# One-hot operations set apart in the attention's step, block factors written in two halves

## The chip, the core and the metric

The kernel runs on one core of a Trainium2 chip. The metric is the device time of one execution in microseconds (us). The engines work in parallel, each on its own queue in order, and meet by semaphores: TensorE multiplies, VectorE and ScalarE compute elementwise, GpSimd issues the gathers here, and SyncE issues the other transfers.

## The reference

Four graph layers follow each other on 3125 nodes of 128 features and 53125 edges, sorted by their destination `dst`. Each layer's output is added to its input and normalised:

```python
x = _layernorm(x + _L0_gnn_ref(x, edge_index, edge_type_16, ...))   # 2 bases
x = _layernorm(x + _L1_gnn_ref(x, src, dst, edge_type_32, ...))     # two layers, 4 bases each
x = _layernorm(x + _L2_gnn_ref(x, edge_index, W, b))                # sum of neighbours, linear, relu
x = _layernorm(x + _L3_gnn_ref(x, Wq, bq, ..., src, dst))           # attention, 8 heads

# inside L1, for each of its two layers:
msg = sum(comp[l][etype][:, b:b+1] * (h[src] @ basis[l, b]) for b in range(4))
h = tanh(segment_sum(msg, dst) + h @ loop_w[l] + bias[l])

# inside L3:
s = einsum('edh,edh->eh', q[row], k[col])
p = exp(s - segment_max(s, row)[row]);  attn = p / segment_sum(p, row)[row]
out = segment_sum(attn * v[col], row)
```

## The kernel before

The edges lie in 416 chunks of 128. The kernel runs three passes of edge sums (the first for L0, the second and the third for the two layers of L1; L2 is made of edge counts that the passes also collect) and then the attention. Times of the trace: first pass to about 540 us, second from 545 to 965, third from 965 to 1390, attention from 1460 on.

**A pass.** GpSimd fetches the source rows of a chunk by one indirect DMA (line 748), two chunks to a group, into a ring of 26 slots (G). VectorE writes for each chunk the scatter factors S (line 1404: position of the edge's destination in a window of 24, times the edge's coefficient for each base). TensorE multiplies G by S into `p_g` (line 815, `sums`), and VectorE adds that to `agg` (line 1431, `add`). A slot of G is refilled after its `sums` (GpSimd waits on `s_mm`).

The second and third passes are "mixed": of every 16 groups 12 are gathered this way, and the edges of the other four are handled as a block. For each of 13 blocks, 14 buckets of edges are picked out of the node table in SBUF by TensorE (line 931) and copied by ScalarE (line 1174). For each bucket VectorE writes the block factors `Sb` (lines 1434 to 1441, `block_factor`): four bases of a window of 72, 288 values to a partition, from the constant row `con` (places 1 to 72), the bucket's place `row[:, PAY - 2]` and its four coefficients. TensorE multiplies (line 944, `block_sum`), which increments `s_bs2`. `Sb` is a ring of 4. That makes 182 block factors in a pass, 364 in all.

VectorE's order in a step i of a pass (`sums_body`, one step a group): add of group i-3, block add where a block ends, count adds (line 1522), scatter factors of group i, block factors of step i+1, key one-hots for the counts (line 1508), and in the third pass residual, normalisation, splits and dense adds (line 1598) instead of the counts. TensorE's order: bucket fetch, block sums of step i, sums of group i-1, counts, transposes and products of finished tiles, in the third pass dense products (line 873).

**The attention** takes 26 batches of 16 chunks, each in four quarters of 4 chunks. GpSimd gathers key and value rows of a chunk (line 2021) into a ring of 64; it refills a slot when the quarter's `values` is done. VectorE multiplies queries and keys (`products`, line 2275), sums by head (`head_part`, line 2281), makes running maxima over a segment (`chunk_max`, `row_max`, `segment_max`), weighs the values (`values`, line 2334), and adds window sums to `agg` (`add`, line 2362). For the window sums TensorE needs the one-hot of each edge's place in a window of 40, `oh1`, a ring of 5 batches. `one_hots(k)` writes those of batch k in four operations of 4 chunks each, in step k-2, one right behind the other. Each increments `s_oh1`, and TensorE's `window_sums(q)` of batch k reads them in step k+2.

All the order is written out in the program; no scheduler rearranges it.

## Time and profile before

| | us |
|---|---|
| median of 3 runs | 2023.86 (2019.08 to 2028.87) |
| the profiled execution | 2026.14 |
| its span, first to last instruction | 2024.3 |
| TensorE busy (matmuls) | 1611.5 (80%) |
| VectorE busy | 1555.9 (77%) |
| GpSimd busy | 1440.2 (71%) |
| ScalarE busy | 1070.8 (53%) |

Busy times add up over stages with different limits, and a busy share says little of what sets the end. GpSimd is counted busy while it makes the descriptors of a gather, not in the 0.30 us of issue between two. Instructions on VectorE overlap a little at their ends, so a group's busy time is less than its count times its mean. The mean of the granted TensorE clock is 0.737 of full speed; it is 0.50, the lower level of 1.2 GHz, through the attention, and near 1 in the second and third passes.

### The profile page before, as it was taken

What the parts mean: (1) busy time and instruction counts of PE and PEld (TensorE: products, weight loads), DVE (VectorE), ACT (ScalarE), POOL (GpSimd) and SP (SyncE); (2) the same over time, 40 slices, a digit from 0 to 9 for tenths busy, and PEclk for the clock granted to TensorE, in tenths of its full rate; (3) what the DMA queues carried; (4) which work ended last, traced back from release to release, by engine and by line L of the source; (5) the groups of instructions that cost most, each with busy time, mean ns of one, the idle gap of its engine ahead of it and who ended that gap; (6) DMA issues with size and microseconds to landing.
All of it is one profiled execution on the core that took longest, in us unless ns stands there. A gap on an engine that the chain in (4) does not pass through costs nothing.

```text
span 2024.3 us, 36062 instructions
## 1 busy us (share of the span) xinstructions
PE 1611.5 (80%) x10129; PEld 1326.4 (66%) x10160; DVE 1555.9 (77%) x4756; ACT 1070.8 (53%) x2202; POOL 1440.2 (71%) x1482
## 2 busy tenths in 40 slices
PE   3988888888589888898399999997628777677777
PEld 2766776667477777777387877774417656566666
DVE  7886767767679888898477777777859877777786
ACT  3355646555588677666466655552464343434341
POOL 6777777777577777776677777772277777777772
PEclk9566566665699999999699999999855555555555
DMA  6232232323133333433534343432286555555551
GB/s 184 56 89 78 66 89 56 88 57 88 51 103 100 104 105 103 132 103 88 155 76 131 111 134 105 130 105 90 85 222 175 162 169 154 163 158 161 161 147 45
DMA packets 171435, 231.75 MB, mean 114 GB/s; under 512 B 48220, under 2 KB 123983, under 8 KB 170980
## 3 DMA queue, kind: packets, MB, share of 16 engines
q0 software_dynamic: 53376, 123.02, 22.0%
q1 hardware_dynamic: 116710, 104.76, 17.5%
q8 instruction: 86, 1.41, 0.3%
q10 hardware_dynamic: 1154, 1.67, 0.3%
q14 instruction: 109, 0.89, 0.1%
HBM read 196.52 MB, written 36.08 MB: 115 GB/s over the span
## 4 chain that ended last, share of the span: by engine, by line
PE 20%; POOL 18%; issue 7%; DVE 6%; DMA 3%; ACT 2%; SPq 1%; DVEq 0%; POOLq 0%; ACTq 0%
POOL G L2021 17%; PE p_d L944 4%; PE p_d L873 4%; PE p_g L931 4%; PE p_g L815 3%; DMA G<-kv_d,idx 2%; PE p_o L858 2%; DMA G<-h_d,idx 1%; POOL G L748 1%; DVE hs L2281 1%; PE p_w L2081 1%; SPq L694 1%; ACT agg L1215 1%; PE p_o L853 1%; DVE XH L2275 0%
## 5 line engine op out<-in xcount | busy, mean ns | idle before, releaser
L748 POOL DMA_INDIRECT G<-h_d,idx x624 | 619.9, 993 | 217.9 <-issue 179.5
L2021 POOL DMA_INDIRECT G<-kv_d,idx x416 | 405.1, 974 | 162.6 <-issue 158.0
L748 POOL DMA_INDIRECT G<-in_x,idx x416 | 400.5, 963 | 131.4 <-issue 111.2
L815 PEld LDWEIGHTS p_g<-S,G 128*128 128x128 f32 x2080 | 352.9, 233 | 163.9 <-issue 96.3
L815 PE MATMUL p_g<-S,G 128*128 128x96 f32 (+1 forms) x2080 | 372.4, 314 | 102.2 <-DMA G<-in_x,idx 56.9
L1404 DVE SCALAR_TENSOR_TENSOR S<-con,rel,shared 128x96 f32<-128x96 f32 (+1 forms) x1040 | 262.3, 294 | 0.4
L1182 ACT ACTIVATE work<-con,lo_f 128x128 bf16<-128x128 f32 x416 | 143.1, 392 | 206.7 <-PE p_d L827 206.6
L1431 DVE TENSOR_TENSOR agg<-agg,p_g 128x96 f32 (+1 forms) x520 | 119.7, 230 | 158.9 <-PE p_g L815 143.1
L944 PE MATMUL p_d<-Sb,kv_s 128*128 128x288 f32 x728 | 220.2, 420 | 20.6 <-ACT kv_s L1174 13.2
L1522 DVE TENSOR_TENSOR work<-work,p_d 128x312 f32 (+1 forms) x416 | 180.2, 465 | 58.1 <-PE p_d L827 52.1
L2081 PE MATMUL p_w<-oh,PV 128*128 128x40 f32 x832 | 195.1, 410 | 24.4 <-DVE PV L2334 23.2
L1508 DVE TENSOR_SCALAR work<-iota_h,key_f 128x600 bf16<-128x600 f16 x416 | 212.8, 522 | 0.0
L2081 PEld LDWEIGHTS p_w<-oh,PV 128*128 128x128 f32 x832 | 187.7, 331 | 31.9 <-DVE PV L2334 26.3
L827 PE MATMUL p_d<-work 128*128 128x312 bf16 (+1 forms) x832 | 187.3, 359 | 0.2 <-DVE work L1522 0.2
L1439 DVE SCALAR_TENSOR_TENSOR Sb<-con,slots 128x288 f32<-128x288 f32 x364 | 174.1, 514 | 11.1 <-PE p_d L944 11.1
L944 PEld LDWEIGHTS p_d<-Sb,kv_s 128*128 128x128 f32 x728 | 127.5, 195 | 48.1 <-ACT kv_s L1174 18.2
L2275 DVE TENSOR_TENSOR XH<-p_qe,G 128x512 f32<-128x512 f32 x104 | 71.3, 686 | 80.0 <-DMA G<-kv_d,idx 76.4
L931 PE MATMUL p_g<-XH,hot 128*128 128x128 f32 x728 | 93.7, 283 | 45.7 <-ACT hot L1167 45.7
L827 PEld LDWEIGHTS p_d<-work 128*128 128x128 bf16 x832 | 103.3, 135 | 30.5 <-issue 2.1
L931 PEld LDWEIGHTS p_g<-XH,hot 128*128 128x128 f32 x728 | 89.8, 198 | 48.2 <-issue 27.0
L1174 ACT ACTIVATE kv_s<-p_g 128x512 f32<-128x512 f32 (+1 forms) x104 | 55.8, 536 | 113.2 <-PE p_g L931 113.0
L2281 DVE TENSOR_REDUCE hs<-XH 128x32 f32<-128x512 f32 x104 | 110.8, 1065 | 2.7
(338 smaller groups left out, 2950.9 us busy)
## 6 DMA issues: line engine op xcount, KB each, us to landing
dst_b<-in_dst_row SPq DMA_DIRECT2D x104, 240.0 KB, 3.2
work<-A_d SPq DMA_DIRECT2D x25, 800.0 KB, 5.7
A_d<-work SPq DMA_DIRECT2D x12, 1600.0 KB
G<-h_d,idx POOLq DMA_INDIRECT x624
G<-in_x,idx POOLq DMA_INDIRECT x416
kv_s<-low_d SPq DMA_DIRECT2D x52, 128.0 KB
G<-kv_d,idx POOLq DMA_INDIRECT x416, 3.3
kv_s<-low_d SPq DMA_DIRECT2D x52, 96.0 KB
```

The lines of the kernel that those rows point to most:

```text
L748: pool.indirect_dma_start(G[:, n % GRING, :], None, l.table, bass.IndirectOffsetOnAxis(ap=l.places[:, c:c + 1], axis=0)).then_inc(s_arr[i ...
L815: last = pe.matmul(p_g[:, g % PB, 0:width], G[:, c % GRING, :], S[:, c % (SRING * GR), 0:width], start=(k == 0), stop=(k == GR - 1))
L827: last = pe.matmul(p_d[:, 1 + half, 0:(hi - lo) * W], lows[:, slot, :], keys[:, slot, lo:hi, :], start=(k == 0), stop=(k == GR - 1))
L931: last = pe.matmul(p_x[:, k * P:(k + 1) * P], hots[n % 2][:, t % 2, k, :], l.x_in[:, t, :], start=(t == tiles[0]), stop=(t == tiles[-1]))
L944: pe.matmul(p_s[:, 0:l.nb * WB], picked[:, n % 2, at:at + P], Sb[:, m % SBR, 0:l.nb * WB], start=(k == 0), stop=(k == GRP - 1)).then_inc(s ...
L1182: last = act.activation(lows[:, slot + k, :], con[:, C_I:C_I + P], ACT.Square, bias=lo_f[:, c:c + 1], scale=1.0)
L1404: last = dve.scalar_tensor_tensor(S[:, slot + k, 0:l.nb * W].rearrange("p (b w) -> p b w", w=W), bc(iota, 1, l.nb), rel[:, c:c + 1], bc(co ...
L1439: dve.scalar_tensor_tensor(Sb[:, m % SBR, 0:l.nb * WB].rearrange("p (b w) -> p b w", w=WB), bc(con[:, C_I + 1:C_I + 1 + WB], 1, l.nb), row ...
L1508: dve.tensor_scalar(keys[:, slot], iota_h[:].rearrange("p (t w) -> p t w", w=W), key_f[:, c:c + 1], None, ALU.is_equal).then_inc(s_hot, 1)
L1522: dve.tensor_tensor(place, place, p_d[:, 1 + half, 0:(hi - lo) * W].rearrange("p (t w) -> p t w", w=W), ALU.add).then_inc(s_bad, 1)
L2021: pool.indirect_dma_start(G[:, c % KRING, :], None, d["kv"], bass.IndirectOffsetOnAxis(ap=idx[:, c:c + 1], axis=0)).then_inc(s_arr[c // QC ...
L2081: pe.matmul(p_w[:, q % 2, 0:WA], PV[:, q % VRING, c, :], oh1[:, k % OH1, j * QC + c, :], start=(c == 0), stop=(c == QC - 1))
```

## The change

Two edits, both on VectorE. In `block_factor` the one operation over all four bases becomes a loop of two operations over two bases each; the second carries the semaphore. In the attention `one_hots(k, some)` takes the numbers of the quarters to write, and the step calls it four times: where it stood, before `products(4k+1)`, before `segment_max`, and after `head_part(4k+2)`. The other engines' programs stay as they are, but for line numbers.

```diff
@@ block_factor
             f, row = l.f0 - 2, slots[:, i, k, :]
-            dve.scalar_tensor_tensor(Sb[:, m % SBR, 0:l.nb * WB].rearrange("p (b w) -> p b w", w=WB),
-                                     bc(con[:, C_I + 1:C_I + 1 + WB], 1, l.nb), row[:, PAY - 2:PAY - 1],
-                                     bc(row[:, f:f + l.nb], 2, WB), ALU.is_equal, ALU.mult).then_inc(s_Sb, 1)
+            for b in range(0, l.nb, 2):
+                last = dve.scalar_tensor_tensor(Sb[:, m % SBR, b * WB:(b + 2) * WB].rearrange("p (b w) -> p b w", w=WB),
+                                                bc(con[:, C_I + 1:C_I + 1 + WB], 1, 2), row[:, PAY - 2:PAY - 1],
+                                                bc(row[:, f + b:f + b + 2], 2, WB), ALU.is_equal, ALU.mult)
+            last.then_inc(s_Sb, 1)
@@ one_hots
-        def one_hots(k):
+        def one_hots(k, some):
             if k >= OH1:
                 dve.wait_ge(s_mm, 4 * (k - OH1 + 1))
-            for j in range(4):
+            for j in some:
@@ the attention's step
                 if batch(k + 2):
-                    one_hots(k + 2)
+                    one_hots(k + 2, (0,))
                 if old:
                     add(4 * k - 7)
                     values(4 * k - 5)
+                if batch(k + 2):
+                    one_hots(k + 2, (1,))
                 if now:
                     products(4 * k + 1, landed)
                     head_part(4 * k + 1)
+                if batch(k + 2):
+                    one_hots(k + 2, (2,))
                 if mid:
                     segment_max(k - 1)
...
                 if now:
                     products(4 * k + 2, landed)
                     head_part(4 * k + 2)
+                if batch(k + 2):
+                    one_hots(k + 2, (3,))
                 if old:
                     add(4 * k - 5)
```

VectorE in a step of the attention before, from the copies that end the row maximum (L2313) on; `oh` is `oh1`, `agg<-agg,p_w` the add, `PV` the values, `XH<-p_qe,G` the products, `hs` the head sums, `FB` the scans:

```order
L2313 COPY R<-fut 1x8
L2268 TENSOR_TENSOR oh<-con,rel 128x160 x4
L2362 ISA
L2362 TENSOR_TENSOR agg<-agg,p_w 128x2x40
L2334 TENSOR_TENSOR PV<-G,p_bk 128x512
L2275 TENSOR_TENSOR XH<-p_qe,G 128x512
L2281 TENSOR_REDUCE hs<-XH 128x32
L2292 SCALAR_TENSOR_TENSOR FB<-shared,ic,p_sT 128x128
L2293 SCALAR_TENSOR_TENSOR FB<-shared,ic,p_sT 128x128
L2320 TENSOR_TENSOR M<-FB 128x128
L2322 TENSOR_TENSOR Dt<-p_sT,M 128x128
```

The same stretch of the changed kernel (its lines are 2 further on):

```order
L2315 COPY R<-fut 1x8
L2270 TENSOR_TENSOR oh<-con,rel 128x160
L2364 ISA
L2364 TENSOR_TENSOR agg<-agg,p_w 128x2x40
L2336 TENSOR_TENSOR PV<-G,p_bk 128x512
L2270 TENSOR_TENSOR oh<-con,rel 128x160
L2277 TENSOR_TENSOR XH<-p_qe,G 128x512
L2283 TENSOR_REDUCE hs<-XH 128x32
L2270 TENSOR_TENSOR oh<-con,rel 128x160
L2294 SCALAR_TENSOR_TENSOR FB<-shared,ic,p_sT 128x128
L2295 SCALAR_TENSOR_TENSOR FB<-shared,ic,p_sT 128x128
L2322 TENSOR_TENSOR M<-FB 128x128
```

The second one-hot moved behind the values, the third behind the head sums; the fourth, after these rows, moved behind the next head sums. No neighbour of a one-hot is another one.

VectorE in a step of the second pass before; `S` are the scatter factors, `Sb` the block factors, `work<-iota_h,key_f` the key one-hots:

```order
L1522 TENSOR_TENSOR work<-work,p_d 128x12x24
L1404 SCALAR_TENSOR_TENSOR S<-con,rel,shared 128x96 x2
L1508 TENSOR_SCALAR work<-iota_h,key_f 128x25x24
L1431 ISA
L1431 TENSOR_TENSOR agg<-agg,p_g 128x4x24
L1404 SCALAR_TENSOR_TENSOR S<-con,rel,shared 128x96 x2
L1439 SCALAR_TENSOR_TENSOR Sb<-con,slots 128x288 x2
L1508 TENSOR_SCALAR work<-iota_h,key_f 128x25x24
```

And in the changed kernel:

```order
L1524 TENSOR_TENSOR work<-work,p_d 128x12x24
L1404 SCALAR_TENSOR_TENSOR S<-con,rel,shared 128x96 x2
L1510 TENSOR_SCALAR work<-iota_h,key_f 128x25x24
L1431 ISA
L1431 TENSOR_TENSOR agg<-agg,p_g 128x4x24
L1404 SCALAR_TENSOR_TENSOR S<-con,rel,shared 128x96 x2
L1440 SCALAR_TENSOR_TENSOR Sb<-con,slots 128x144 x4
L1510 TENSOR_SCALAR work<-iota_h,key_f 128x25x24
```

Each block factor is now two neighbouring instructions of half the width, and nothing changed its place.

## Rows read from the trace of the kernel before

**Rows 1.** The page's header, and its chain of waits by line.
```profile
span 2024.3 us, 36062 instructions
...
POOL G L2021 17%; PE p_d L944 4%; PE p_d L873 4%; PE p_g L931 4%; PE p_g L815 3%; DMA G<-kv_d,idx 2%; PE p_o L858 2%; DMA G<-h_d,idx 1%; POOL G L748 1%; DVE hs L2281 1%; PE p_w L2081 1%; SPq L694 1%; ACT agg L1215 1%; PE p_o L853 1%; DVE XH L2275 0%
```

**Rows 2.** Gathers: second pass, third pass, attention; then their lines' shortest/median/longest.
```profile
L748 POOL DMA_INDIRECT G<-h_d,idx x312 | 312.7, 1002 | 107.1 <-issue 90.2 <-DVEq L1841 12.3 <-PE p_g L815 4.6
...
L748 POOL DMA_INDIRECT G<-h_d,idx x312 | 307.2, 984 | 110.8 <-issue 89.3 <-DVEq L1841 16.0 <-PE p_g L815 5.5
...
L2021 POOL DMA_INDIRECT G<-kv_d,idx x416 | 405.1, 974 | 162.6 <-issue 158.0 <-DVE PV L2334 4.6
...
L748 POOL DMA_INDIRECT G<-h_d,idx x624: 940/944/2102, 544.7 to 1369.2; - x156
...
L2021 POOL DMA_INDIRECT G<-kv_d,idx x416: 942/946/1997, 1459.6 to 1990.2; - x139
```

**Rows 3.** Timeline of GpSimd in the attention: start, us, instruction, idle before.
```profile
1716.86 0.95 POOL L2021 DMA_INDIRECT G<-kv_d,idx  x1 [0.30 <-issue]
...
1902.77 1.72 POOL L2021 DMA_INDIRECT G<-kv_d,idx  x1 [0.30 <-issue]
...
1943.59 1.32 POOL L2021 DMA_INDIRECT G<-kv_d,idx  x1 [0.30 <-issue]
```

**Rows 4.** Timeline of VectorE at the same places: runs of four one-hots.
```profile
1717.13 1.01 DVE L2268 TENSOR_TENSOR oh<-con,rel 128x160 f32<-128x160 f32 x4
...
1902.65 1.01 DVE L2268 TENSOR_TENSOR oh<-con,rel 128x160 f32<-128x160 f32 x4
...
1943.08 1.01 DVE L2268 TENSOR_TENSOR oh<-con,rel 128x160 f32<-128x160 f32 x4
```

**Rows 5.** The chain of waits, from the last gather on.
```profile
1990.23 2.72 DMA G<-kv_d,idx
...
1993.04 0.70 DVE XH L2275
```

**Rows 6.** Timeline of GpSimd in the second pass.
```profile
678.46 1.04 POOL L748 DMA_INDIRECT G<-h_d,idx  x1 [0.31 <-issue]
...
758.66 0.94 POOL L748 DMA_INDIRECT G<-h_d,idx  x1 [0.31 <-issue]
...
839.68 1.18 POOL L748 DMA_INDIRECT G<-h_d,idx  x1 [0.30 <-issue]
```

**Rows 7.** Timeline of VectorE at the same places.
```profile
678.38 0.54 DVE L1404 SCALAR_TENSOR_TENSOR S<-con,rel,shared 128x96 f32<-128x96 f32 x2
678.84 0.94 DVE L1439 SCALAR_TENSOR_TENSOR Sb<-con,slots 128x288 f32<-128x288 f32 x2
...
758.42 0.54 DVE L1404 SCALAR_TENSOR_TENSOR S<-con,rel,shared 128x96 f32<-128x96 f32 x2
...
839.53 0.94 DVE L1439 SCALAR_TENSOR_TENSOR Sb<-con,slots 128x288 f32<-128x288 f32 x2
840.38 0.53 DVE L1508 TENSOR_SCALAR work<-iota_h,key_f 128x600 bf16<-128x600 f16 x1
```

**Rows 8.** Groups on VectorE: factors and one-hots (page), scatter factors of the second pass.
```profile
L1439 DVE SCALAR_TENSOR_TENSOR Sb<-con,slots 128x288 f32<-128x288 f32 x364 | 174.1, 514 | 11.1 <-PE p_d L944 11.1
...
L2268 DVE TENSOR_TENSOR oh<-con,rel 128x160 f32<-128x160 f32 x104 | 26.3, 307 | 0.0
...
L1404 DVE SCALAR_TENSOR_TENSOR S<-con,rel,shared 128x96 f32<-128x96 f32 x312 | 84.9, 315 | 0.1
```

**Rows 9.** Stretches: start:end, us, then busy us (instructions) of each engine.
```profile
600.00:690.00 90.00, 84.23 (x597) 72.89 (x596) 86.06 (x266) 70.95 (x145) 69.20 (x69) 1.00 0.35 90
690.00:790.00 100.00, 86.15 (x575) 73.38 (x573) 85.07 (x257) 73.18 (x142) 76.31 (x78) 0.95 0.42 119
...
965.00:1390.00 425.00, 379.48 (x2443) 307.97 (x2472) 308.77 (x1039) 237.25 (x355) 307.16 (x312) 0.95 0.39 118
```

**Rows 10.** Waits of TensorE in the second pass: in total, times, longest.
```profile
PE p_d L944 <- DVE Sb L1439: 5.2, 14, 0.8
```

## The prediction

> **What bounds the kernel now.** I read the chain of waits first. Its largest line is GpSimd's gather of the attention, 17% of the span, and no other line comes near [rows 1]. Then the groups of gathers, stretch by stretch. A gather has a median of 0.944 us (0.946 in the attention) and some 0.30 us of issue behind it, and the idle time before gathers is put almost wholly to issue: in the second pass 90.2 us of 107.1, with 12.3 at the pass's start and 4.6 put to TensorE [rows 2]. So GpSimd issues one gather behind the other without waiting for buffers: 312 in some 407 us per later pass (1.29 us each), 416 in the attention (1.28 us each). In the attention the end hangs on the last one: it lands after 2.72 us, the product starts 0.09 us later, and the tail behind it holds no one-hot [rows 5]. A microsecond that GpSimd loses or gains there is one of the time.
>
> The means are above the medians: 1.002 us in the second pass, 0.984 in the third, 0.974 in the attention [rows 2]. That is 312 × 0.058 = 18.1 us, 312 × 0.040 = 12.5 us and 416 × 0.028 = 11.6 us of lengthened gathers. The timelines show beside what. The gather of 1902.77 took 1.72 us, and the run of four one-hots (1902.65, 1.01 us) ended at 1903.66; the gather of 1943.59 took 1.32 us, the run ended at 1944.09; that of 1716.86 took 0.95 us though a run began at 1717.13 and lay over most of it [rows 3, 4]. So a gather needs something once, 0.12 us after its start, and if VectorE is then inside such a run, it waits to the run's end: 1903.66 - 1902.89 = 0.77, against 1.72 - 0.95 = 0.77; 1944.09 - 1943.71 = 0.38 against 0.37. Most gathers lie beside VectorE's products, scans and sums, and keep the median of 0.946 us [rows 2]. In the second pass a block factor does it too: gather 839.68 grew by 0.24 us, and from 839.80 to the first factor's end (839.53 + 0.51) are 0.24 [rows 6 to 8]. Scatter factors (line 1404) do it less: gather 678.46 grew by 0.10 us, from 678.58 to the end of the first of the two (678.38 + 0.31), not of the second; gather 758.66 did not grow, though its instant lay 0.13 us inside the second [rows 6, 7]. So with these scalar_tensor_tensor operations a gather slips in between two neighbours, and each holds from some 0.12 us after its start only. The run of one-hots held as one.
>
> The Trainium skill ("SBUF — State Buffer", "Who interferes with whom") says that a VectorE instruction with two inputs in SBUF contends with a GpSimd instruction that reads SBUF, and infers that writing descriptors does not suffer. By its inference the lengthened gathers would not exist; the trace disagrees, with 1.72 us for 0.95. Elsewhere on that page the hold is of the whole instruction; gather 758.66, not delayed at 0.13 us into a factor, says less. By the page a half would hold 0.36 us, two of them as often as one of 0.51, and the passes' term below would be nothing.
>
> **Part one, the attention.** 96 of the 104 one-hots stood in 24 runs of four (8 more stand in one run ahead of the first product, unchanged). A gather comes each c us, so its instant falls into a hold of h us with chance h/c and waits h/2 on average: h²/2c for each hold. For a run that is 1.01²/(2 × 1.28) = 0.40 us, for 24 runs 9.6 us, of the 11.6 us above. Now each stands alone between a row scan's copies, a value product, a head sum or a score sum, which do not hold. One lasts 0.307 us [rows 8] and holds at most all of that, at least 0.19 us (with a factor's lead-in of 0.12); I take 0.26: 0.26²/2.56 = 0.026 us, 96 times 2.5 us. Gain 7.1 us, bounded by 9.6 (no one-hot is ever hit: VectorE's phase is tied to the landings, so the four places can be lucky) and by 2 (two of the four places always hit at 0.15 us, 24 × 2 × 0.15 = 7.2 us left). VectorE's work does not grow; the first is still behind row_max, the others later by up to some 8 us (of 20 us a step), and TensorE reads them two steps on, so no wait opens. What was behind the run (add, values, products) comes up to 0.7 us sooner, which only lengthens the wait for the gather. I take -7.
>
> **Part two, the block factors.** 364 operations of 128x288 become 728 of 128x144. Starts of neighbours: 288 wide 0.85/2 = 0.43 us, 96 wide 0.46/2 = 0.23 us [rows 7], so 1.04 ns an element over 0.13 us fixed. 144 wide: 0.28 us from start to start, 0.36 us long (0.315 + 48 × 1.04 ns) [rows 8]. Two are 0.56 us against 0.43: 0.13 us more per factor, 23.7 us of VectorE in each later pass. On the other side GpSimd: a factor held 0.41 us (0.51 less 0.10; with 0.12 it would be 0.39, and 10.7 us below for 11.9), 0.41²/(2 × 1.29) = 0.065 us, 182 times 11.9 us a pass; two halves hold 0.24 us each, 0.022 us, 364 times 8.1 us. Gain 3.8 us a pass.
>
> Does the added 23.7 us lie beside other work? In the second pass VectorE was busy 86.06 of 90 us and then 85.07 of 100 [rows 9]. At 0.058 us per us (23.7/407) the first stretch gets 5.2 us for 3.9 idle ones, the second 5.8 for 14.9. So it falls behind by a microsecond or two and catches up where TensorE is late for its own reasons, if the idle time can be used. It is close: TensorE already waited 14 times for a block factor, 5.2 us [rows 10]. Behind a late half on VectorE stand the key one-hots, the count sums and the next add; TensorE's block sum waits for it, and behind that the gathered sums and the ring that GpSimd refills. Bounds: the pass ends 3.8 us earlier (all absorbed) or 23.7 us later (none); nearest is the row of idle time, so a debt of some 4 us at the end, near nothing net: I take +1. In the third pass VectorE was busy 308.77 of 425 us and TensorE 379.48 [rows 9]; the 23.7 us find cover, but TensorE bounds part of it, so of GpSimd's 3.8 us I count 1.5 (bounds -4 and +5).
>
> **Sum.** -7 + 1 - 1.5 = -7.5 us. The profiled execution took 2026.1 us (span 2024.3 [rows 1] and 1.8 around it), so 2018.6 by it; its runs have a median of 2023.9, 2.3 lower, so 2016.4 by that. I say 2017 us.
>
> **Rivals.**
> - VectorE's work takes over in the second pass (chance 0.16). From the point where it has no idle time left in any 100 us, some 15 us of debt, the pass is VectorE's and the gain of GpSimd's is void there. For it: 96% busy with the addition (182.1 of the first 190 us), and the 14 waits. Against: the 14.9 idle us in the second stretch, and a gather ring that runs ahead. With 20 of the 23.7 us paid: 20 - 7 - 1.5 = +11.5, 2037 by the profile, 2035 by the median.
> - The halves hold as one, since nothing waits between them (0.07). Then the hold is 0.28 + 0.36 - 0.12 = 0.52 us, 0.105 us per factor against 0.065: 364 × 0.04 = 14.6 us more on GpSimd. For it: the one-hots did, with no wait between. Against: the scatter pair of 678.38, no wait between, let the gather in. -7 + 15 + 1 = +9: 2033.
> - The change does not do what it would: halves hold from their start, so the passes gain nothing and keep a small debt (0.12): -7 + 3 = -4, 2020. A fourth, that gathers are longer for a reason of their own and neither edit reaches them: +3, 2029 by the profile, 2027 by the median (0.03); against it stand the two runs of one-hots, each fitting to 0.01 us. It is what the Trainium skill's inference on descriptors ("SBUF — State Buffer", "Who interferes with whom") comes to here.
> - Lucky phases (0.17): -9.5 in the attention, the debt wholly absorbed: -9.5 - 3 - 2 = -14.5, 2010.
> - My forecast, 0.45.
>
> A difference under 0.5% (10 us) cannot be told from none here; the three runs alone span 9.8 us. Faster by more: the lucky case and a quarter of the forecast, 0.29. Slower by more: most of the first rival and half of the second, 0.17. Within: 0.54. The range for 8 in 10 reaches from 2007 (lucky, and a run at the low end) to 2034 (the first rival nearly whole); my own case alone is 2010 to 2024.
>
> **What would show it.** Attention: gathers' mean down from 0.974 to about 0.953 us, none above 1.3 beside a one-hot, first to last gather some 7 us shorter. Passes: 0.36 us and 0.28 us apart for a half; means down from 1.002 and 0.984 by some 0.012 us; VectorE busy some 24 us more in each. The forecast is wrong if the second pass lasts over 5 us longer, if gathers beside pairs of halves wait 0.5 us, or if the attention's mean stays.

## The result: 0.5% slower, by longer gathers in the later passes

The changed kernel takes 2033.26 us (median of 7 runs, 2031.45 to 2036.68) against 2023.88 (7 runs, 2019.08 to 2028.87), a ratio of 1.0047 with a 95% interval of 1.0033 to 1.0062. I had forecast 2017 us. The measured time lies just inside the range (2007 to 2034), but on the other side of no change.

**The profile after.** The header and the chain of waits by line, of the changed kernel:

```profile
span 2030.6 us, 36426 instructions
...
POOL G L2023 19%; PE p_d L944 4%; PE p_d L873 4%; POOL G L748 3%; PE p_g L931 3%; PE p_g L815 3%; PE p_o L858 1%; DMA G<-h_d,idx 1%; DMA G<-kv_d,idx 1%; SPq L694 1%; PE p_w L2083 1%; ACT agg L1215 1%; PE p_o L853 0%; PE p_d L827 0%; DVE XH L1792 0%
```

The attention's gather still leads the chain. The passes' gather, L748, rose from 1% [rows 1] to 3%. The groups of gathers by stretch (second pass, third pass, attention) answer to [rows 2]:

```profile
L748 POOL DMA_INDIRECT G<-h_d,idx x312 | 320.2, 1026 | 106.9 <-issue 90.6 <-DVEq L1843 12.1 <-PE p_g L815 4.3
...
L748 POOL DMA_INDIRECT G<-h_d,idx x312 | 311.2, 997 | 110.3 <-issue 88.7 <-DVEq L1843 15.5 <-PE p_g L815 6.1
...
L2023 POOL DMA_INDIRECT G<-kv_d,idx x416 | 400.8, 963 | 162.8 <-issue 161.2 <-DVE PV L2336 1.5
```

The idle time before the gathers is what it was (106.9 for 107.1 us, 110.3 for 110.8, 162.8 for 162.6). Only their own time changed: +7.5 us in the second pass, +4.0 in the third, -4.3 in the attention. The sum, +7.2, answers to 2030.6 - 2024.3 = 6.3 us of span. In what follows I call the busy time of a group over 0.944 us for each gather its *excess*: 320.2 - 312 × 0.944 = 25.7 us here in the second pass, against 18.2 before, and in the attention 400.8 - 392.7 = 8.1 against 12.4 (the prediction took 0.946 us there, hence its 11.6).

What the longer gathers lie beside is seen in the timelines. GpSimd in the second pass:

```profile
750.48 1.87 POOL L748 DMA_INDIRECT G<-h_d,idx  x1 [0.30 <-issue]
...
753.90 1.12 POOL L748 DMA_INDIRECT G<-h_d,idx  x1 [0.31 <-issue]
```

and VectorE at the same places:

```profile
750.33 1.20 DVE L1440 SCALAR_TENSOR_TENSOR Sb<-con,slots 128x144 f32<-128x144 f32 x4
751.44 0.52 DVE L1510 TENSOR_SCALAR work<-iota_h,key_f 128x600 bf16<-128x600 f16 x1
...
753.56 1.20 DVE L1440 SCALAR_TENSOR_TENSOR Sb<-con,slots 128x144 f32<-128x144 f32 x4
```

Both gathers meet a run of four halves, whose ends lie 0.36, 0.64, 0.92 and 1.20 us after the run's start. The instant of the gather of 753.90, 0.12 us after its start, is 754.02, in the second half; that half ends at 754.20, and the gather is 1.12 - 0.94 = 0.18 us longer. That is the rule of the prediction. The instant of 750.48 is 750.60, in the first half, which ends at 750.69. But the gather is 0.93 us longer, up to 751.53, the end of the whole run. It was held through the three halves that it had not met. In the second pass of before none was: I counted 67 gathers that were longer beside block factors, and each ended its wait at the end of the factor that it met (excess together 15.9 us). In the changed kernel 67 were longer beside halves, 35 ended at the end of their own half (4.1 us in all), and 32 at a later one (18.9 us).

One gather of before, in the third pass, was held on in the same way. It is the longest of line 748, the 2102 ns that end that line's row in [rows 2]:

```profile
978.74 2.10 POOL L748 DMA_INDIRECT G<-h_d,idx  x1 [0.30 <-issue]
```

```profile
978.62 0.54 DVE L1404 SCALAR_TENSOR_TENSOR S<-con,rel,shared 128x96 f32<-128x96 f32 x2
979.08 0.94 DVE L1439 SCALAR_TENSOR_TENSOR Sb<-con,slots 128x288 f32<-128x288 f32 x2
```

Its instant is 978.86, and it is 2.10 - 0.94 = 1.16 us longer, up to 980.02. That is the end of the second whole factor (979.08 + 0.94). The first scatter factor had ended at 978.93, and it was held through three more neighbours.

**VectorE's added work cost nothing.** Busy time of VectorE in three stretches of the second pass, before (the last of its rows) and after:

```profile
790.00:890.00 100.00, 89.08 (x273) 0.97 0.37 103
```

```profile
600.00:690.00 90.00, 86.43 (x292) 1.00 0.36 89
690.00:790.00 100.00, 93.80 (x314) 0.95 0.44 117
790.00:890.00 100.00, 87.47 (x293) 0.95 0.37 102
```

With [rows 9] that is 260.2 us before and 267.7 after of 290. These are stretches of fixed length, and the changed kernel gets through less of the pass in them. Over the whole program VectorE was busy 1600.4 us for 1555.9, so some 22 us more in each later pass. The waits of TensorE for block factors grew in the second pass from 5.2 us, 14 times [rows 10], to 11.2 us, 19 times. Over the whole program they grew from 7.2 us, 17 times, to this row:

```profile
PE p_d L944 <- DVE Sb L1440: 12.8, 23, 1.5
```

But the gathers did not wait for it, and the next pass began as soon after the last gather as before (15.5 us for 16.0, the DVEq share of the rows above).

**The attention.** One of the one-hots that now stand alone, with the gather beside it:

```profile
1750.21 1.07 POOL L2023 DMA_INDIRECT G<-kv_d,idx  x1 [0.30 <-issue]
```

```profile
1750.14 0.32 DVE L2270 TENSOR_TENSOR oh<-con,rel 128x160 f32<-128x160 f32 x1
1750.37 0.48 DVE L2294 TENSOR_TENSOR_SCAN FB<-shared,ic,p_sT 128x128 f32<-128x128 f32 x1
```

The instant, 1750.33, is 0.13 us before the one-hot's end, and the gather is 0.13 us longer. The scan behind it does not hold it. That is the predicted effect.

### The profile page after: what moved, and what is told of

The parts are those of the page before. It is cut to its first block, busy times and chain, and to the rows that moved or that the text cites. A ratio compares the mean times of both kernels' runs of the same rounds, so it can differ in the third digit from the quotient of the medians.

```text
span 2030.6 us, 36426 instructions
## 1 busy us (share of the span) xinstructions
PE 1611.7 (79%) x10129; PEld 1316.2 (65%) x10160; DVE 1600.4 (79%) x5120; ACT 1070.5 (53%) x2202; POOL 1448.0 (71%) x1482
## 4 chain that ended last, share of the span: by engine, by line
POOL 22%; PE 17%; issue 8%; DVE 4%; DMA 2%; ACT 2%; SPq 1%; DVEq 0%; POOLq 0%; ACTq 0%
POOL G L2023 19%; PE p_d L944 4%; PE p_d L873 4%; POOL G L748 3%; PE p_g L931 3%; PE p_g L815 3%; PE p_o L858 1%; DMA G<-h_d,idx 1%; DMA G<-kv_d,idx 1%; SPq L694 1%; PE p_w L2083 1%; ACT agg L1215 1%; PE p_o L853 0%; PE p_d L827 0%; DVE XH L1792 0%
## 5 line engine op out<-in xcount | busy, mean ns | idle before, releaser
L748 POOL DMA_INDIRECT G<-h_d,idx x624 | 631.4, 1012 | 217.2 <-issue 179.3
L2023 POOL DMA_INDIRECT G<-kv_d,idx x416 | 400.8, 963 | 162.8 <-issue 161.2
L748 POOL DMA_INDIRECT G<-in_x,idx x416 | 401.3, 965 | 131.6 <-issue 109.8
L944 PE MATMUL p_d<-Sb,kv_s 128*128 128x288 f32 x728 | 220.5, 420 | 23.7 <-DVE Sb L1440 12.8
L1440 DVE SCALAR_TENSOR_TENSOR Sb<-con,slots 128x144 f32<-128x144 f32 x728 | 220.5, 360 | 10.4 <-PE p_d L944 10.3
L2283 DVE TENSOR_REDUCE hs<-XH 128x32 f32<-128x512 f32 x104 | 110.8, 1066 | 2.7
```

What stands on the lines that cost most here:

```text
L748: pool.indirect_dma_start(G[:, n % GRING, :], None, l.table, bass.IndirectOffsetOnAxis(ap=l.places[:, c:c + 1], axis=0)).then_inc(s_arr[i ...
L944: pe.matmul(p_s[:, 0:l.nb * WB], picked[:, n % 2, at:at + P], Sb[:, m % SBR, 0:l.nb * WB], start=(k == 0), stop=(k == GRP - 1)).then_inc(s ...
L1440: last = dve.scalar_tensor_tensor(Sb[:, m % SBR, b * WB:(b + 2) * WB].rearrange("p (b w) -> p b w", w=WB), bc(con[:, C_I + 1:C_I + 1 + WB] ...
L2023: pool.indirect_dma_start(G[:, c % KRING, :], None, d["kv"], bass.IndirectOffsetOnAxis(ap=idx[:, c:c + 1], axis=0)).then_inc(s_arr[c // QC ...
```

## Experiments

The theory before the first of them: a gather that waits beside short two-input operations is held through neighbours too, so halves cost more than wholes (rival 2 in part). Against it: VectorE's added work, and an effect of the attention's edit on the passes. The ratios are to runs of the kernel before on the same chip, made beside them. e8, e10, e11, e12 and e13 have one run each (2068.9, 2032.1, 2020.0, 2051.6 and 2026.0 us), so for them I read the excess and not the time.

**e1, the attention's edit alone.** The one-hots in four places, block factors whole.

> Only the one-hots stand apart; the block factors are one operation each, as before. Hold theory (a gather waits for VectorE operations with two SBUF inputs, and GpSimd sets the pace): the attention's stretch from first to last gather falls from 531.5 to about 527 us, the passes stay at 407.5 and 401.9, total 4 to 6 us below before, ratio 0.997 to 0.998. VectorE theory (added VectorE work in the passes made the change slower, and the one-hots do nothing): ratio 1.000.

Measured: 2014.88 us (12 runs), ratio 0.9963 (0.9950 to 0.9977), so -7.5 us. Its group in the attention:

```profile
L2021 POOL DMA_INDIRECT G<-kv_d,idx x416 | 399.2, 960 | 162.6 <-issue 160.8 <-DVE PV L2334 1.8
```

The attention's excess is 6.5 us for 12.4. The profiled execution's span is 12.2 us below that of before (2012.1 for 2024.3): 5.9 us of it are these gathers, and 3.9 us those of the second pass (excess 14.3), whose code is that of before. So the same code differs by some 4 us there from one profile to another, and a term of that size can't be read from one profile.

**e2, the block factors alone.** The two operations a factor, one-hots in one run.

> Only the block factors are halved. Hold theory with halves that hold on into each other: second pass 407.5 to about 415 us from first to last gather, third 401.9 to about 406, the attention at 531.5, the stretches between the last gather of a pass and the first of the next unchanged; total 11 to 14 us above before, ratio 1.006 to 1.007. VectorE theory: the same total, but it shows behind the last gather of a pass or as gathers that wait for TensorE, not as longer gathers.

Measured: 2036.93 us (6 runs), ratio 1.0078 (1.0059 to 1.0097), so +15.8 us. The second and the third pass:

```profile
L748 POOL DMA_INDIRECT G<-h_d,idx x312 | 315.8, 1012 | 106.9 <-issue 89.3 <-DVEq L1843 12.1 <-PE p_g L815 5.5
L748 POOL DMA_INDIRECT G<-h_d,idx x312 | 309.2, 991 | 112.3 <-issue 89.6 <-DVEq L1843 17.5 <-PE p_g L815 5.2
```

The product of the two ratios is 1.0041, and both edits together gave 1.0047. The loss is that of the halves. But this profile shows only a part of it: its span is 9.7 us above that of before (2034.0 for 2024.3), the excess grew by 3.1 and 2.1 us, and from first to last gather the two passes grew by 3.4 and 2.1 us, where I had expected some 7.5 and 4. Means over several profiles are a better measure. With whole factors (before, e1, e4, e5, e7) the excess is 15.1 us in the second pass and 11.8 in the third, with halves (after, e2, e10) 24.3 and 15.5. That is 13.0 us more, inside the interval of e2's time (11.9 to 19.6 us).

**e3, block factors by one-input operations.** `tensor_scalar` compares and multiplies with two values that each partition has of its own, so it has one tensor input.

```diff
-            dve.scalar_tensor_tensor(Sb[:, m % SBR, 0:l.nb * WB]..., bc(con[...], 1, l.nb), row[:, PAY - 2:PAY - 1],
-                                     bc(row[:, f:f + l.nb], 2, WB), ALU.is_equal, ALU.mult)
+            for b in range(l.nb):
+                last = dve.tensor_scalar(Sb[:, m % SBR, b * WB:(b + 1) * WB], con[:, C_I + 1:C_I + 1 + WB],
+                                         row[:, PAY - 2:PAY - 1], row[:, f + b:f + b + 1], ALU.is_equal, ALU.mult)
```

> Each block factor is four tensor_scalar operations of one base (72 wide) with one SBUF tensor input, the place and the coefficient being scalars by pointer; the attention as before. VectorE gets at least as much more work as by the halving (four starts instead of one). Hold theory, if one-input operations do not hold: the passes' gathers lose the 13.8 and 7.7 us that they wait beside block factors, second pass to about 394, third to about 394 us, total 15 to 20 us below before, ratio 0.990 to 0.993. VectorE theory: total at least 9 us above before. If a one-input fp32 operation holds as well, the gathers grow to means above 1.03 us and the ratio is above 1.005.

Measured: ratio 1.0416 (1.0394 to 1.0439). The second pass, and its factors:

```profile
L748 POOL DMA_INDIRECT G<-h_d,idx x312 | 297.7, 954 | 137.4 <-issue 81.1 <-PE p_g L815 43.8 <-DVEq L1842 12.5
...
L1440 DVE TENSOR_SCALAR Sb<-con,slots 128x72 f32<-128x72 f32 x1456 | 352.6, 329 | 8.9 <-PE p_d L944 8.9
```

The excess fell from 18.2 to 3.2 us: these one-input operations hardly hold a gather (0.7 us of it ends at one of them, and 2.0 at scatter factors). The time missed what was expected (0.990 to 0.993) by far. They bring VectorE 0.48 us more per factor (four of 0.23 against one of 0.43), and now it is the bound: GpSimd waits 43.8 us for sums in this pass, and 44.2 us instead of 16.0 before the third pass begins.

**e4, one-hots by one-input operations.** In the attention, 16 operations of 40 values a batch, in one run; block factors whole.

```diff
-                dve.tensor_tensor(oh1[:, k % OH1, j * QC:(j + 1) * QC, :], bc(iota, 1, QC),
-                                  bc(rel[:, c:c + QC], 2, WA), ALU.is_equal).then_inc(s_oh1, 1)
+                for n in range(QC):
+                    last = dve.tensor_scalar(oh1[:, k % OH1, j * QC + n, :], iota, rel[:, c + n:c + n + 1], None,
+                                             ALU.is_equal)
+                last.then_inc(s_oh1, 1)
```

> Only the attention's one-hots change: each operation of 4 chunks becomes four tensor_scalar operations of one chunk (40 wide) with one SBUF tensor input, all of a batch still in one run. Hold theory, if one-input operations do not hold: the 9.3 us that gathers wait beside the one-hots vanish, the attention's stretch falls from 531.5 to about 522 us, ratio 0.995 to 0.996, though VectorE works some 0.8 us more a batch. If they hold as the run did, the run is longer and the stretch grows to about 540 us, ratio 1.004.

Measured: 2011.85 us (6 runs), ratio 0.9955 (0.9939 to 0.9971). The attention:

```profile
L2021 POOL DMA_INDIRECT G<-kv_d,idx x416 | 397.0, 954 | 162.6 <-issue 162.0 <-DVE PV L2336 0.6
```

The excess is 4.3 us, lower than with the one-hots apart (6.5).

**e5, VectorE's added work alone.** Whole block factors, and behind each a tiny one-input operation.

```diff
+            dve.tensor_scalar(idle_t[:, m % 24:m % 24 + 1], con[:, C_ONE:C_ONE + 1], 1.0, None, ALU.mult)
```

> The kernel before, with its whole block factors of 288 values, and behind each factor one tiny one-input operation of VectorE over a single column, into a buffer that nothing reads. VectorE gets some 0.06 to 0.13 us more per factor, 11 to 24 us in each later pass, the work that the halves add; the holds stay those of before. Theory 1 (VectorE's added work is what the passes paid for): the second and the third pass grow by some 7 and 4 us as in the changed kernel, the time comes out some 9 to 13 us over before, ratio 1.005 to 1.006. Theory 2 (longer gathers, because a gather is held through more than one half): passes within 2 us of before's 407.5 and 401.9, lengthened gathers still some 18 and 12 us, those beside block factors 14 and 8 us, ratio 0.999 to 1.001.

Measured: 2023.28 us (12 runs), ratio 1.0009 (1.0000 to 1.0019). The second pass, and VectorE in the three stretches:

```profile
L749 POOL DMA_INDIRECT G<-h_d,idx x312 | 312.3, 1001 | 107.0 <-issue 91.4 <-DVEq L1843 12.2 <-PE p_g L816 3.4
```

```profile
600.00:690.00 90.00, 84.49 (x294) 1.00 0.36 89
690.00:790.00 100.00, 91.08 (x317) 0.95 0.46 120
790.00:890.00 100.00, 92.14 (x320) 0.97 0.38 103
```

84.49 + 91.08 + 92.14 = 267.7 us, as busy in these stretches as in the changed kernel, and the excess is 17.8 us, that of before. Over the whole program, though, VectorE was busy 1575.5 us, so e5 added 19.6 us where the halves added 44.5, and it is only a part of the control. The full one is e14 against e4 below: 45.3 us more of VectorE's work there (1634.9 for 1589.6), and the same ratio to before (0.9953 and 0.9955). So the load is not the cause.

**e6, something between the halves.** The changed kernel with the same tiny operation behind each half.

```diff
                 last = dve.scalar_tensor_tensor(Sb[...two bases...], ..., ALU.is_equal, ALU.mult)
+                dve.tensor_scalar(idle_t[:, ...:... + 1], con[:, C_ONE:C_ONE + 1], 1.0, None, ALU.mult)
```

> The changed kernel with the same tiny one-input operation behind each half of a block factor (1 column), so that no half has another half as its neighbour; VectorE's work grows again, some 0.13 to 0.25 us per factor. Theory 1 (the gather that waits misses the short step from one half to the next and is held through the neighbour; an operation that holds nothing in between lets it in): lengthened gathers beside block factors fall from 19.4 and 11.8 us in the changed kernel's second and third pass to some 8 and 5 us (a single half's hold of 0.24 us by 364), and no gather beside them is over 1.25 us but for the copies' sake; the passes then last what VectorE allows, 405 to 415 us. Theory 2 (a half holds longer for itself, or the halves meet the gathers in a bad phase): still 17 us or more in the second pass. Theory 3 (VectorE's work is the cost): the second pass well over 415 us.

Measured: ratio 1.0062 (1.0046 to 1.0079). The second and the third pass:

```profile
L749 POOL DMA_INDIRECT G<-h_d,idx x312 | 301.5, 966 | 106.9 <-issue 90.2 <-DVEq L1846 12.2 <-PE p_g L816 4.6
L749 POOL DMA_INDIRECT G<-h_d,idx x312 | 302.9, 971 | 132.1 <-issue 90.5 <-DVEq L1846 37.3 <-PE p_g L816 4.3
```

The excess fell from 25.7 to 7.0 us and from 16.7 to 8.4, and of 50 lengthened gathers beside halves in the second pass none waited past its own half. The pass is 11 us shorter than before. One such gather, and what VectorE did:

```profile
748.96 1.05 POOL L749 DMA_INDIRECT G<-h_d,idx  x1 [0.30 <-issue]
```

```profile
748.84 0.36 DVE L1441 SCALAR_TENSOR_TENSOR Sb<-con,slots 128x144 f32<-128x144 f32 x1
749.11 0.14 DVE L1446 TENSOR_SCALAR idle_t<-con 128x1 f32<-128x1 f32 x1
749.18 0.36 DVE L1441 SCALAR_TENSOR_TENSOR Sb<-con,slots 128x144 f32<-128x144 f32 x1
```

The instant is 749.08, its half ends at 749.20, and the gather is 0.11 us longer; the next half, begun at 749.18, does not hold it. The load does cost here: in the three stretches VectorE was busy 88.1, 99.4 and 96.5 us, and the third pass began 37.3 us after the last gather instead of 15.5. That is why the time is no better.

**e7, one-input one-hots, also apart.** e4 with the four places of the change.

> The one-hots of the attention as 16 one-input operations a batch (tensor_scalar, iota against one edge's place), as in e4, and also set apart in four places of the step as in the changed kernel; block factors whole. Theory 1 (a one-input operation holds no gather, so where it stands is of no matter): as e4, ratio to before 0.9955 within its interval, lengthened gathers of the attention 4 to 5 us, first to last gather 523 to 525 us. Theory 2 (standing apart has a worth of its own, what stood behind the run comes sooner): 2 us or more below e4.

Measured: 2010.36 us (6 runs), ratio 0.9952 (0.9938 to 0.9966), excess of the attention 3.1 us (395.8 - 392.7). It can't be told from e4: once a one-hot holds next to nothing, its place is of no matter that these runs can show.

**e8, quarters.** One base to an operation, four a factor.

```diff
-            for b in range(0, l.nb, 2):
+            for b in range(0, l.nb):
```

> The changed kernel with each block factor as four neighbouring two-input operations of 128x72 (one base each). Estimate from the starts of neighbours: 0.20 to 0.21 us apart, 0.29 us long, so some 0.39 us more of VectorE per factor than before, about the same work as in e6 (two halves and two tiny operations). Theory 1 (a gather that waits may be held through the next neighbour where nothing that holds nothing stands between): lengthened gathers beside block factors stay at the changed kernel's 19.4 us in the second pass or grow, single ones wait up to 1.6 us, all in all 26 us or more against e6's 7.0, though VectorE's work is that of e6; the second pass 415 us or more. Theory 2 (e6's short gathers came from VectorE's later phase, not from what stands between): below 12 us in all.

```profile
L748 POOL DMA_INDIRECT G<-h_d,idx x312 | 302.4, 969 | 119.0 <-issue 85.9 <-PE p_g L815 20.8 <-DVEq L1843 12.3
```

Theory 1 fell in its simple form. The excess is 7.9 us, and of 61 lengthened gathers one waited past its quarter, though up to eight stand in a row. So it is not enough that neighbours are short. (VectorE was busy 99.4 of 100 us in two stretches here, so the gathers did meet it in other phases.)

**e9, something between the halves of a factor only**, with e4's one-hots; a second half still has the next factor's first half behind it.

> The one-hots of the attention as one-input operations (e4), and block factors in halves with one tiny one-input operation between the two halves of a factor only; the second half still has the next factor's first half as its neighbour. VectorE gets some 0.27 us more per factor. Theory 1 (held through a neighbour): the longest chain is of two halves, so lengthened gathers of the second pass are between e6's 7.0 and e4's 12.1 us, say 9, and of the third 9 for 12; VectorE's added 49 us a pass are mostly covered (e5 hid 26 us a pass, e6's 73 us made the next pass begin 22 us later): start of the third pass 0 to 8 us later. Ratio to before 0.994 to 1.000, so at best level with e4. Theory 2 (two neighbours chain as often as four): second pass over 12 us lengthened.

Measured: 2018.42 us (10 runs), ratio 0.9984 (0.9971 to 0.9997). Excess 7.8 and 8.9 us, about the 9 and 9 expected, and none of 55 lengthened gathers of the second pass held on. Only 3 of them (8 in the third pass) had met a half with another right behind it, so e9 says little of such a pair. The third pass began 26.2 us after the last gather, 10 us later than before and not 0 to 8. It is slower than e4: as in e6, the load takes the gain back.

**e10, halves cut the other way**: four bases by 36 places, instead of two bases by 72.

> The changed kernel with the halves cut the other way: all four bases over 36 places of the window, instead of two bases over all 72. Same number of operations, the same 144 values each, other strides. Theory 1 (what counts is that two short neighbours stand without a gap): as the changed kernel, lengthened gathers of the second pass 21 to 26 us, of the third 14 to 17. Rival (the shape of the pieces, [2,72], has to do with the release): clearly below 20 in the second pass.

```profile
L748 POOL DMA_INDIRECT G<-h_d,idx x312 | 320.5, 1027 | 107.1 <-issue 89.9 <-DVEq L1844 12.3 <-PE p_g L815 4.9
```

Excess 26.0 us; 37 of 67 lengthened gathers held on. The shape of the pieces made no difference.

**e11, an uneven cut.** The changed kernel with one base, then three: 72 and 216 values, as many operations and as much work as the halves.

```diff
-            for b in range(0, l.nb, 2):
+            for b, n in ((0, 1), (1, 3)):
```

> The changed kernel with its factor cut unevenly: one operation over one base (72 values, estimate 0.20 us to the next start, from the quarters) and one over three (216 values, some 0.36 us to the next start, 0.43 long). Count of operations and VectorE's work are those of the halves. Theory 1 (it is the equal step of 0.28 us of the halves at which a waiting gather misses one neighbour's edge after the other; the quarters' 0.20 us and the pairs of whole factors do not do it): lengthened gathers of the second pass fall from 25.7 us to some 15 to 19, of the third from 16.7 to 12 to 14. Theory 2 (any two neighbours of this kind chain about every second time once a piece is 144 values or longer, whatever the steps): 20 us or more in the second pass, gathers held from the long piece through the next factor's pieces.

```profile
L748 POOL DMA_INDIRECT G<-h_d,idx x312 | 305.9, 980 | 107.8 <-issue 88.7 <-DVEq L1843 13.0 <-PE p_g L815 6.1
```

Excess 11.4 us against 25.7 with halves; 7 of 49 lengthened gathers held on (1.5 us together), and these ended some 0.08 us past the operation that they met, at no neighbour's end.

**e12, thirds**: four bases by 24 places, 96 values, three operations a factor.

> The changed kernel with its factor as three operations of four bases by 24 places of the window (96 values each; the scatter factors of that size start 0.23 us apart and last 0.315 us), 0.26 us more of VectorE per factor than before. Theory 1 (chains come at the step of 0.28 us only) and the simple rule by size (pieces below 144 values let the gather in at each edge, as the quarters of 72 did): 8 to 12 us lengthened in the second pass, no gather beside them over 1.25 us. Theory 2 (the quarters are the exception): 20 us or more. With VectorE's added work as in e9 the time comes out at some 2020 to 2035 us by either.

```profile
L748 POOL DMA_INDIRECT G<-h_d,idx x312 | 332.1, 1065 | 107.1 <-issue 89.3 <-DVEq L1844 12.3 <-PE p_g L815 5.5
```

The highest excess of all, 37.6 us; 41 of 86 held on, and they bring 30.9 us. Both theories' time (2020 to 2035 us) was missed with it. The rule by size that I had set beside theory 1 (the smaller, the more harmless) fell with it. A gather and its run of six:

```profile
775.87 1.72 POOL L748 DMA_INDIRECT G<-h_d,idx  x1 [0.31 <-issue]
```

```profile
775.30 1.46 DVE L1441 SCALAR_TENSOR_TENSOR Sb<-con,slots 128x96 f32<-128x96 f32 x6
```

Its instant is 775.99, and 775.99 + 0.78 is 776.77, the run's end.

**e13, a nearly equal cut**: four bases by 32 and by 40 places, 128 and 160 values.

> The changed kernel with its factor cut into four bases by 32 and by 40 places (128 and 160 values; starts some 0.26 and 0.30 us apart), the VectorE work of the halves. Theory 1 (gathers are held on only where the neighbours' steps are one and the same, 0.28 us or 0.23 us): lengthened gathers of the second pass 10 to 16 us, as with the uneven cut (11.3). Theory 2 (pieces of some 0.3 to 0.37 us hold a gather on, equal or not; only pieces well off that, 0.29 and 0.44 us, don't): 19 to 27 us, as the halves (25.7).

```profile
L748 POOL DMA_INDIRECT G<-h_d,idx x312 | 317.3, 1017 | 107.3 <-issue 87.8 <-DVEq L1844 12.5 <-PE p_g L815 7.0
```

Excess 22.8 us; 26 of 59 held on. So the steps need not be equal (theory 2): pieces of a block factor of some 0.31 to 0.38 us hold on, those of 0.29 and those of 0.44 hardly.

**e14, the uneven cut with e4's one-hots.**

> The one-input one-hots of e4 (in one run) and the uneven block factors of e11 (one base, then three). Theory 1 (the uneven cut holds no gather on, VectorE's added 0.13 us per factor costs nothing): lengthened gathers of the second pass 10 to 13 us, of the third 10 to 13, attention 4 to 5; the time within 4 us of e4, ratio to before 0.9935 to 0.9965. Rival (e11's 11.3 us was luck of one execution): 18 us or more in the second pass, ratio 0.998 or above.

Measured: 2012.22 us (6 runs), ratio 0.9953 (0.9937 to 0.9969).

```profile
L748 POOL DMA_INDIRECT G<-h_d,idx x312 | 305.1, 978 | 106.9 <-issue 89.6 <-DVEq L1843 12.1 <-PE p_g L815 5.2
```

Excess 10.6 us, 6 of 49 held on: e11 was no luck. In time it is level with e4 and e7, though VectorE has 45.3 us more to do than in e4. The three are the fastest versions found, each about 0.5% below before; of them e4 changes least.

All that was measured of block factors, by the second pass (starts and lengths from the rows' means and the timelines; held on: lengthened gathers that waited past the end of the operation that they met):

| block factor as | step, length, us | excess, us | held on, of lengthened |
|---|---|---|---|
| one of 288 (before, e1, e4, e5, e7) | 0.43, 0.51 | 18.2, 14.3, 12.2, 17.8, 12.9 | 0 of 67 (before) |
| two of 144 (after, e2, e10) | 0.28, 0.36 | 25.7, 21.3, 26.0 | 32 of 67, 29 of 54, 37 of 67 |
| 128 + 160 (e13) | 0.26 and 0.30, 0.34 and 0.38 | 22.8 | 26 of 59 |
| three of 96 (e12) | 0.23, 0.31 | 37.6 | 41 of 86 |
| 72 + 216 (e11, e14) | 0.20 and 0.35, 0.29 and 0.44 | 11.4, 10.6 | 7 of 49, 6 of 49 |
| four of 72 (e8) | 0.20, 0.29 | 7.9 | 1 of 61 |
| 144 with a tiny one-input one between (e6, e9) | 0.34 or 0.28, 0.36 | 7.0, 7.8 | 0 of 50, 0 of 55 |

The last column counts every lengthened gather, also those that met an operation with no two-input neighbour right behind it and so could not be held on. Without these, over both passes, and with the operation begun last before the instant as the one met, a count of the traces gives: halves (after, e2, e10) 120 held on of 279; 128 + 160 31 of 90; thirds 60 of 107; whole factors (before, e1, e4, e7) 2 of 108; quarters none of 37; uneven none of 65 (without those that ended 0.08 us past their operation). In the changed kernel it is 32 of 52 in the second pass and 8 of 43 in the third. Scatter factors have the size, the length and the step of the thirds, and beside them only 1 of 606 such gathers was held on, in all 16 kernels together: the gather of 978.74.

## Why the prediction was wrong

**What bounds the kernel: right.** GpSimd's issue of gathers set the time of the later passes and of the attention. A microsecond of excess was about one of time from first to last gather, with gaps nearly unchanged, until VectorE ran out of slack (e3, e6, e8, e9).

**Part one, -7 us: right.** e1 gave -7.5 us (interval -10.1 to -4.7), with one profile showing 5.9 us as shorter gathers in the attention (4.3 in the changed kernel's). Over the trace, 9.3 us of excess had stood beside one-hots before and some 3.5 are left in e1, against 9.6 and 2.5 in the working. I had expected a mean of about 0.953 us and it was 0.963 and 0.960. The 0.953 was a slip: the working's own 7.1 us give 0.974 - 7.1/416 = 0.957.

**Part two, VectorE's cost: right in size, and covered.** A half lasts 0.36 us and starts 0.28 us after its neighbour, as worked out, and VectorE's 44.5 us more over both passes answer to 2 × 23.7. The debt that I put at +1 us, and the first rival at +20, came to nothing: e14 has 45.3 us more of VectorE's work than e4 and the same ratio to before (0.9953 and 0.9955). What rival 1 describes does exist, at about twice the work: in e6 VectorE was busy 84.2 us more than before (1640.1 us), 284.0 of 290 in the three stretches, and the next pass began 22 us late.

**Part two, GpSimd's gain: the step that failed.** It is the sentence "with these scalar_tensor_tensor operations a gather slips in between two neighbours, and each holds from some 0.12 us after its start only", carried over from [rows 6, 7] to halves. The second half of it holds (timelines above, e6). The first was read from one pair of whole factors and one of scatter factors. For both kinds it is nearly always true (table and count above); for pieces of 144 values it failed in 32 of 52 cases in the second pass and in 8 of 43 in the third. In place of 3.8 us less excess per pass there were 7.5 and 4.1 us more. Had the gathers always slipped in, about the excess of e6 might have been left, 7.0 and 8.4 us, as far as its phases are those of the changed kernel. The term had a smaller fault besides: it takes a lead-in of 0.10 us from a whole factor and 0.12 from a half. With 0.12 for both the gain is 10.7 - 8.1 = 2.6 us a pass, not 3.8.

**The rival that came out** is the second, "the halves hold as one", to which I gave 0.07, with 2033 us. Its total was right and its mechanism half so: it charged every factor with a hold of 0.52 us, +14.6 us over both passes, where only some of the gathers are held on, but then mostly to the end of all halves in the row, not only of their own pair: +11.6 us in this profile. The gather of 986.43, in the third pass, took 2.61 us: it was held through two scatter factors and the four halves behind them. The evidence for this rival stood in the profile. The one-hots at 0.31 us, the one run of short neighbours that had been looked at closely, did hold as one, and the longest gather of line 748, the 2102 ns in [rows 2] that the working does not touch, is the one held through three neighbours at 978.74. Against it I had set one gather beside a pair of scatter factors. With such evidence on both sides the chance of 0.07 was too low.

**The rival that the gathers are longer for a reason of their own** is refuted by e3, e4 and e6. The Trainium skill ("SBUF — State Buffer", "Who interferes with whom") says that a VectorE instruction with at most one SBUF input, outside the 2-port modes, does not contend with GpSimd; the traces agree, with 3.2 us of excess left in e3 and 4.3 in e4's attention, though no row shows in which mode these `tensor_scalar` operations ran. Its inference that descriptor writing isn't held up by `tensor_tensor` does not stand here.

**What stays open.** Why a waiting gather misses the edge between neighbours of 0.31 to 0.38 us about every second time, and, once it has missed one, mostly all up to the next operation that holds nothing, and why it hardly does at 0.29, 0.44 and 0.51 us. That something between ends it (e6) is shown, and so is that for block factors the size of the pieces matters and not their shape (e10), their equality (e13) or VectorE's load (e11, e14). But size is not the whole of it: scatter factors of 96 values let the gather in nearly always, thirds of 96 values do not. Whether the phase in which GpSimd meets VectorE has a part in it, no run here tests. A mechanism is not shown. Nor do I know what sets the phase by which the same whole factors cost 12.2 us in one kernel and 18.2 in another.

## What to carry to other kernels

Where a queue of descriptor-writing gathers sets the pace, first look for VectorE operations with two tensor inputs in SBUF, and turn them into one-input forms where VectorE has the slack (e4: -0.45%, in three lines); if they must stay, stand them apart between one-input ones. Look up the longest gather in the trace, and what it lies beside, before trusting a rule read from typical ones. Cutting such an operation into short neighbours can lengthen the holds instead of shortening them: compare the gathers' excess, and not the length of one operation. A rule read from two or three rows of one size is a rule for that size.

## What the runs showed of the hardware that I had not expected

- A gather that meets a two-input VectorE operation can be held through three neighbours that it had not met: beside pieces of a block factor of 96 to 160 values often (0.93 us in the changed kernel; 0.78 in the row of e12), beside pieces of 72, 216 and 288 values and beside scatter factors of 96 almost never (978.74 is one such case; table and count above).
- One operation over a single column between them, 0.14 us long and some 0.07 us of VectorE's time, ends that wholly (e6: 0 of 50).
- One-input `tensor_scalar` operations of 72 or 40 float32 values hold next to nothing (e3, e4), but cost 0.23 and 0.15 us from start to start, so four of them take 0.48 us more than one two-input operation of 288 values.
